# A post-norm decoder layer on one core: x1 turned by DMA, the last two feed-forwards turned by TensorE, steps ordered anew

## The reference

```
# linear attention, 16 heads of 64, 32 features
q' = exp((x Wq + bq) wq_feat);  k' = exp((x Wk + bk) wk_feat);  v = x Wv + bv
a  = q' (k'^T v) / (q' sum(k') + 1e-6);   x1 = layernorm(x + a Wproj + bproj)
# cross attention, 16 heads of 8, keys and values from the context
x2 = layernorm(x1 + softmax((x1 Wq'^T + bq')(ctx Wk'^T + bk')^T / sqrt(8)) (ctx Wv'^T + bv') Wo^T + bo)
# feed-forward 128 -> 512 -> 128 with ternary weights
h  = gelu(x2 ternary(W_fc)^T);  y = layernorm(x2 + layernorm(h; ln_w, ln_b) ternary(W_proj)^T)
```

## Time and profile before

| | us |
|---|---|
| median of 3 runs | 743.17 (742.66 to 746.18) |
| the profiled execution: its time | 746.38 |
| its span, first to last instruction | 742.9 |
| mean granted clock of TensorE | 0.972 of full speed |
| PE, DVE, ACT, POOL busy | 685.4, 527.6, 447.2, 408.5 |

### The profile page before, as it was taken

One profiled execution on the slowest core, in us unless ns is written; L12 is line 12 of the kernel. 1 busy time (PEld: TensorE's weight loads), 2 busy tenths in 40 slices (PEclk: granted clock), 3 DMA queues, 4 the chain that ended last, 5 costly groups with the idle time before them and its releaser, 6 DMA issues.

```text
span 742.9 us, 31000 instructions
## 1 busy us (share of the span) xinstructions
PE 685.4 (92%) x13506; PEld 487.3 (66%) x13506; DVE 527.6 (71%) x1476; ACT 447.2 (60%) x782; POOL 408.5 (55%) x442
## 2 busy tenths in 40 slices
...
GB/s 302 17 45 31 18 31 17 65 50 79 45 31 103 17 116 19 73 54 79 48 31 101 19 107 25 75 45 87 45 25 110 17 75 30 39 53 44 74 56 85
DMA packets 97161, 44.29 MB, mean 60 GB/s; under 512 B 87810, under 2 KB 87939, under 8 KB 96899
## 3 DMA queue, kind: packets, MB, share of 16 engines
...
...
## 4 chain that ended last, share of the span: by engine, by line
PE 72%; POOL 10%; DVE 5%; issue 5%; DMA 5%; ACT 1%; SPq 0%; POOLq 0%; DVEq 0%; ACTq 0%
PE bank L302 12%; PE bank L319 7%; PE bank L292 6%; PE bank L361 4%; DMA x2T<-x2s 4%; POOL gall L931 3%; PE bank L403 3%; PE bank L346 2%; PE bank L388 2%; POOL gs L936 2%; PE bank L315 2%; PE bank L427 2%; PE bank L434 2%; PE bank L435 2%; PE bank L339 2%
## 5 line engine op out<-in xcount | busy, mean ns | idle before, releaser
L931 POOL TENSOR_TENSOR gall<-gall,lnr 128x512 f32<-128x512 f32 x64 | 80.7, 1283 | 85.5 <-DVE st L756 85.5
L302 PE MATMUL bank<-Mh,GT 128*32 128x128 f32 x4096 | 124.4, 273 | 0.3 <-DVE GT L737 0.3
L302 PEld LDWEIGHTS bank<-Mh,GT 128*32 128x32 f32 x4096 | 110.3, 110 | 16.7 <-issue 15.3
L900 POOL TENSOR_SCALAR ve<-mv 128x4 f32<-128x4 f32 x64 | 12.4, 194 | 160.3 <-DVE mv L763 157.5
L786 DVE TENSOR_REDUCE mx<-bank 128x8 f32<-128x512 f32 x128 | 78.1, 681 | 12.6 <-PE bank L361 12.6
L737 DVE COPY GT<-bank 128x512 f32<-128x512 f32 x81 | 52.4, 682 | 36.7 <-PE bank L292 26.4
L936 POOL TENSOR_TENSOR gs<-gall,gs 128x512 f16<-128x512 f32 x64 | 73.4, 1160 | 8.4 <-ACT gs L607 8.1
L580 ACT ACTIVATE PT<-bank 128x512 f32<-128x512 f32 x128 | 64.5, 627 | 8.9 <-PE bank L388 8.9
L903 POOL TENSOR_TENSOR rstd<-ve,mhalf 128x4 f32<-128x4 f32 x64 | 66.9, 1045 | 5.3
L319 PE MATMUL bank<-Cb,qT 128*64 128x128 f32 x1024 | 66.8, 273 | 0.0
L292 PE MATMUL bank<-kp,xs 64*128 64x512 f32 x256 | 63.8, 616 | 0.0
...
## 6 DMA issues: line engine op xcount, KB each, us to landing
...
gT<-gs SPq DMA_TRANSPOSE x64, 2.8
...
```

Of the source, the lines that this page charges most:

```text
L302: m = e.matmul(bk[32 * j:32 * j + 32, tile(g_)], GT[b % 4][:, tile(hh, 32)], Mh[:, tile(hh)], start=True, stop=True)
L931: e.tensor_tensor(g[t][:, :], g[t][:, :], lnr[:, :], ALU.mult).then_inc(s_gs, 1)
```

## The change

x1 is no longer turned by PE, except for group 15. ACT casts x1 to fp16 (x1hi), POOL makes the low half (x1lo), SP turns both with one DMA transpose, and `qproj` is three fp16 matmuls with the query weights split once into halves (`xq`). For groups 14 and 15 x2 and g are turned by PE (`flip3`, and `turn` with four transposes for each of four column blocks); ACT writes the high half out of PSUM, scaled by ln_w, and DVE the low half. `gs`, `gh`, `gl` and the split in `ap2` are gone for these two. The bias that `ap2` added is a step of its own, `ab2`. The order in all three strings is new, as are some of the `+` marks. row1 now lies in a part of PT[0]; ACT's first `prob` also waits for `bias2`. The diff, cut to its core:

```diff
...
 HEAD = """
-small1 wb wk bias2 wq k0@0 k1@0 WkT zeros split@0 k2@0 mh0 g0+@0 g1@0 g2@0 g3@0 mh1 bv q0@0 nbeta q1@0 gam k3@0 small2 c0+@0 c1+@0 ks+@0 c2@0 q2@0
-kst@0 loadx@0 q3@0 WqT g4@0 g5@0 g6@0 g7@0 Wvp c3@0 Wff c4+@0 loadx@1 split@1 c5+@0 dT@0 c6+@0 xb@0 c7+@0 biasA loadc@0 bc0@0 loadx@2 bc1@0 bc2@0 bc3@0
-bias3 sbar
+wb xq wk zeros wq k0@0 small1 k1@0 bias2 q0@0 WkT k2@0 q1@0 k3@0 q2@0 split@0 nbeta gam g0+@0 WqT g1+@0 loadx@0 mh0 mh1 small2 g2+@0 bv Wvp Wff g3+@0
+g4+@0 loadx@1 g5@0 c0+@0 c1@0 ks+@0 loadx@2 c2@0 q3@0 kst@0 biasA g6+@0 g7+@0 dT@0 c3@0 c4@0 loadc@0 c5@0 c6@0 c7@0 bc0@0 split@1 bc1@0 bc2@0 bc3@0
+xb@0 sbar bias3
 PERIOD = """
-k0 k1 down0@4 k2 k3 down1@4 down2@4 score0@2 loadc score1@2 o0@1 o1@1 o2@1 o3@1 rows@2 split@-1 q0 st1@1 q1 down3@4 q2 g0+ ap2@3 g1+ xb g2+ g3 prob0@2
-gs0@3 prob1@2 ks gs1@3 ap1@1 c0+ q3 st3@4 up0@3 up1@3 kst up2@3 gl0@3 up3@3 flip@1 loadx@-2 gh0@3 gl1@3 stat@3 c1+ pv0@2 c2+ dT ap3@4 pv1@2 g4 gh1@3 g5
-g6 g7 qproj@1 kproj@1 ab1@1 gs2@3 oturn0@2 c3 c4+ c5+ c6 gh2@3 c7+ oturn1@2 gs3@3 bc0 bc1 bc2 gl2@3 gl3@3 bc3 cturn0+@2 gh3@3 cturn1+@2 vproj@1 proj0@2
-proj1@2 st2@2
+k0 k1 score0@2 score1@2 o0@1 o1@1 o2@1 o3@1 rows@2 down0@4 st1@1 down1@4 q0 ap2@3 ap1@1 k2 k3 down2@4 down3@4 split@-1 q1 g0 g1+ g2+ x1s@1 g3 st3@4
+gs0@3 prob0@2 prob1@2 gs1@3 ab2@3 ks c0 q2 up0@3 up1@3 up2@3 ap3@4 stat@3 kst up3@3 q3 gh0@3 pv0@2 c1 pv1@2 c2+ c3 dT g4+ gh1@3 g5 g6+ gl0@3 g7 gl1@3
+qproj@1 oturn0@2 gs2@3 kproj@1 oturn1@2 ab1@1 c4 gs3@3 c5 c6+ xb gh2@3 c7 bc0 bc1 bc2 gh3@3 loadx@-2 bc3 gl2@3 cturn0+@2 cturn1+@2 loadc vproj@1
+proj0@2 gl3@3 proj1@2 st2@2
 TAIL = """
...
-gl3@3 ab1@1 rows@1 ap3@4 up0@2 gs0@2 gs1@2 up1@2 up2@2 up3@2 gs2@2 down3@3 prob0@1 prob1@1 gs3@2 gh0@2 pv0+@1 gl0@2 gl1@2 stat@2 gh1@2 pv1@1 oturn0@1
-gl2@2 oturn1@1 cturn0+@1 cturn1+@1 proj0@1 proj1@1 st2@1 gl3@2 down0@2 gh2@2 ap2@1 st3@3 down1@2 gs0@1 gs1@1 gh3@2 down2@2 ap3@3 gl0@1 gl1@1 down3@2
-up0@1 gs2@1 up1@1 up2@1 gh0@1 gs3@1 up3@1 st3@2 gl2@1 gh1@1 gl3@1 stat@1 ap3@2 gh2@1 down0@1 down1@1 down2@1 down3@1 st3@1 gh3@1 ap3@1
...
+down1@3 gl2@3 vproj@1 rows@1 ab2@2 up0@2 up1@2 up2@2 down2@3 up3@2 gl3@3 prob0@1 down3@3 prob1@1 pv0+@1 st3@3 pv1+@1 stat@2 ap3@3 oturn0@1 oturn1@1
+cturn0+@1 cturn1+@1 proj0@1 proj1@1 st2@1 ab2@1 turn0@2 turn1@2 turn2@2 turn3@2 ap2@1 down0@2 down1@2 flip3@1 down2@2 down3@2 up0@1 st3@2 up1@1 up2@1
+stat@1 up3@1 turn0@1 turn1@1 turn2@1 turn3@1 ap3@2 down0@1 down1@1 down2@1 down3@1 st3@1 ap3@1
 """
...
+        flipped = {s for name, s, t, _ in PLAN if name == "flip"}
+        by_pe = sorted({s for name, s, t, _ in PLAN if name == "turn"})
...
+        x1s, x1h = sb("x1s", 1024, F16), x1T[:, :].bitcast(F16)
+        xWqh, xWql = sb("xWqh", 128, F16), sb("xWql", 128, F16)
...
+        gTc = [gTs[:, :].rearrange("p (t h c n) -> p t h c n", t=4, h=2, c=4)[:, :, :, c, :] for c in range(4)]
...
             def qproj(s):
                 bk, done = start("qproj", s)
-                w.wait_ge(*emptied("flip", s))
-                e.matmul(bk[:, :], xWq[:, :], x1T[:, :], start=True, stop=True).then_inc(done, 1)
+                if s in flipped:
+                    w.wait_ge(*emptied("flip", s))
+                    e.matmul(bk[:, :], xWq[:, :], x1T[:, :], start=True, stop=True).then_inc(done, 1)
+                else:
+                    w.wait_ge(s_xql, 1)
+                    w.wait_ge(s_x1T, 16 * (s + 1))
+                    e.matmul(bk[:, :], xWqh[:, :], x1h[:, 0:512], start=True, stop=False)
+                    e.matmul(bk[:, :], xWqh[:, :], x1h[:, 512:1024], start=False, stop=False)
+                    e.matmul(bk[:, :], xWql[:, :], x1h[:, 0:512], start=False, stop=True).then_inc(done, 1)
...
+            def flip3(s):
+                bk, done = start("flip3", s)
+                for t in range(4):
+                    w.wait_ge(s_ln["2"], 4 * s + t + 1)
+                    m = e.transpose(bk[:, tile(t)], x2[s % 2][:, tile(t)], ident[:, :])
+                m.then_inc(done, 1)
+
             def up(s, t):
                 bk, done = start("up", s, t)
                 w.wait_ge(s_prep, 6)
-                w.wait_ge(s_x2T, 16 * (s + 1))
+                if s in by_pe:
+                    w.wait_ge(*emptied("flip3", s))
+                else:
+                    w.wait_ge(s_x2T, 16 * (s + 1))
                 e.matmul(bk[:, :], x2T[:, tile(t)], tfc[:, :], start=True, stop=False)
                 e.matmul(bk[:, :], x2T[:, tile(4 + t)], tfc[:, :], start=False, stop=True).then_inc(done, 1)
 
+            def turn(s, c):
+                bk, done = start("turn", s, c)
+                for t in range(4):
+                    w.wait_ge(*emptied("up", s, t))
+                    m = e.transpose(bk[:, tile(t)], g[t][:, tile(c)], ident[:, :])
+                m.then_inc(done, 1)
+
             def down(s, t):
                 bk, done = start("down", s, t)
-                w.wait_ge(s_gT[t], 16 * (s + 1))
+                if s in by_pe:
+                    for c in range(4):
+                        w.wait_ge(*emptied("turn", s, c))
+                else:
+                    w.wait_ge(s_gT[t], 16 * (s + 1))
...
+            def xq():
+                w.wait_ge(s_small2, 16)
+                e.activation(xWqh[:, :], xWq[:, :], ACT.Copy).then_inc(s_xqh, 1)
+
+            def x1hi(s):
+                w.wait_ge(s_ln["1"], 4 * s + 4)
+                if s > 0:
+                    w.wait_ge(s_x1T, 16 * s)
+                e.activation(x1s[:, 0:512], x1[s % 2][:, :], ACT.Copy).then_inc(s_x1h, 1)
...
+            def flip3(s):
+                if s > 0:
+                    w.wait_ge(*filled("up", s - 1, 3))
+                w.wait_ge(*filled("flip3", s))
+                e.activation(x2T[:, 0:512], bank[uses["flip3", s, 0][0]][:, :], ACT.Copy).then_inc(s_x2hp, 1)
...
+            def turn(s, c):
+                if s > 0:
+                    w.wait_ge(*filled("down", s - 1, 3))
+                w.wait_ge(*filled("turn", s, c))
+                b3 = bank[uses["turn", s, c][0]][:, :].rearrange("p (t n) -> p t n", t=4)
+                e.activation(gTc[c][:, :, 0, :], b3, ACT.Copy, scale=lnw[:, c:c + 1]).then_inc(s_ghp, 1)
...
+                w.wait_ge(s_x2hp, by_pe.index(s) + 1)
+                e.tensor_tensor(x2T[:, 512:1024], bank[uses["flip3", s, 0][0]][:, :], x2T[:, 0:512], ALU.subtract).then_inc(emptied("flip3", s)[0], 1)
...
+            def turn(s, c):
+                w.wait_ge(s_ghp, 4 * by_pe.index(s) + c + 1)
+                b3 = bank[uses["turn", s, c][0]][:, :].rearrange("p (t n) -> p t n", t=4)
+                e.scalar_tensor_tensor(gTc[c][:, :, 1, :], b3, lnw[:, c:c + 1], gTc[c][:, :, 0, :], ALU.mult, ALU.subtract).then_inc(emptied("turn", s, c)[0], 1)
...
+            def x1lo(s):
+                w.wait_ge(s_ln["1"], 4 * s + 4)
+                w.wait_ge(s_x1h, s + 1)
+                e.tensor_tensor(x1s[:, 512:1024], x1[s % 2][:, :], x1s[:, 0:512], ALU.subtract).then_inc(s_x1l, 1)
...
+
+            def ab2(s):
+                if s in by_pe:
+                    w.wait_ge(*filled("flip3", s))
+                    w.wait_ge(s_ln["2"], 4 * s + 4)
+                else:
+                    w.wait_ge(s_x2l, s + 1)
                 w.wait_ge(*emptied("bias3", 0))
-                addbias(x, x, bias3).then_inc(s_x2b, 1)
+                addbias(x2[s % 2], x2[s % 2], bias3).then_inc(s_x2b, 1)
...
+            def x1turn(s):
+                w.wait_ge(s_x1l, s + 1)
+                if s > 0:
+                    w.wait_ge(*filled("qproj", s - 1))
+                e.dma_start(x1h[:, :].rearrange("p (n c) -> p n c", n=8), x1s[:, :], transpose=True).then_inc(s_x1T, 16)
```

More of the change, by code:

```diff
@@ L28 @@
 WIDE = {"score": 4, "prob": 4, "mh": 2}
-BANKED = "k q ks kst dT bc g c o flip kproj vproj qproj score rows prob pv oturn cturn proj up down wq wk wb mh biasA bias2 nbeta gam bias3 sbar".split()
-WHOLE = "small1 small2 ab1 st1 st2 st3 ap1 ap2 ap3 bias2 bias3".split()
+BANKED = "k q ks kst dT bc g c o flip kproj vproj qproj score rows prob pv oturn cturn proj flip3 up turn down wq wk wb mh biasA bias2 nbeta gam bias3 sbar".split()
+WHOLE = "small1 small2 x1s flip3 ab1 ab2 st1 st2 st3 ap1 ap2 ap3 bias2 bias3".split()
@@ L47 @@
[L47 to L50, removed]
@@ L51 @@
-gl3@3 ab1@1 rows@1 ap3@4 up0@2 gs0@2 gs1@2 up1@2 up2@2 up3@2 gs2@2 down3@3 prob0@1 prob1@1 gs3@2 gh0@2 pv0+@1 gl0@2 gl1@2 stat@2 gh1@2 pv1@1 oturn0@1
-gl2@2 oturn1@1 cturn0+@1 cturn1+@1 proj0@1 proj1@1 st2@1 gl3@2 down0@2 gh2@2 ap2@1 st3@3 down1@2 gs0@1 gs1@1 gh3@2 down2@2 ap3@3 gl0@1 gl1@1 down3@2
-up0@1 gs2@1 up1@1 up2@1 gh0@1 gs3@1 up3@1 st3@2 gl2@1 gh1@1 gl3@1 stat@1 ap3@2 gh2@1 down0@1 down1@1 down2@1 down3@1 st3@1 gh3@1 ap3@1
+k0@1 score0@3 ap2@4 score1@3 k1@1 q0@1 o0@2 o1@2 o2@2 o3@2 st1@2 rows@3 gs0@4 q1@1 k2@1 ap1@2 k3@1 up0@4 down0@5 down1@5 x1s@2 up1@4 down2@5 gs1@4
@@ new lines @@
+up2@4 up3@4 g0@1 g1@1 g2+@1 g3@1 down3@5 prob0@3 prob1@3 ab2@4 gl0@4 stat@4 gh0@4 gh1@4 c0+@1 c1@1 st3@5 pv0@3 ks+@1 pv1@3 gs2@4 qproj@2 oturn0@3 q2@1
```

(13 more changed lines are left out.)

58 lines of the change are left out of this document (41 added, 17 removed).

## The result

The changed kernel took 747.49 us (median of 19 runs, 741.68 to 750.76), the kernel before 743.06 (19 runs, 741.54 to 747.19): ratio 1.0051, 95% interval 1.0032 to 1.0070. The forecast of 718.2 us, with a range of 708 to 731, was wrong: the kernel is half a per cent slower and not 3.4% faster.

A forecast was written before the change was run, and what follows sets the result against it. PE's queue was taken to bound the periods, latency the tail; 11.2 + 1.8 - 2.0 + 1.0 + 0.8 + 2.4 + 9.8 = 25.0 us off the profiled 746.38, from the median 718.2 us, range 708 to 731.

The forecast's parts named there:

- x1 by DMA, PE slots: Per group on PE: `flip` and fp32 `qproj` (1.49 us) give way to three fp16 matmuls (0.69); 14 x 0.80 = 11.2 us gained.
- x1's chain costs nothing: Period: x1's halves and DMA transpose land near 18.5 us, `qproj` comes near 28.9; ten microseconds of slack, cost 0.
- x2T waits: Period, PE at `up`: waits for x2T of 3.6 us over five; half taken as gain, 1.8 us, bounds 0 to 3.6.
- (c) of the order: Period: DVE must finish bc products, x2 sums and statistics before the eight maxima; charged 0.15 us a period, +2.0 us, bounds 0 to 14.
- No engine overtakes PE: Period: new loads per group of DVE 34.1, ACT 26.3, POOL 26.5 us stay below a period of 40.9.
- What PE idle costs: Steady periods: time is the sum of PE's slots; DVE lateness was charged in us per period, 0.15, bounds 0 to 1.
- Head: Start of kernel: WqT loaded third, so PE's 0.99 us wait for it goes; gain about 1.0 us, bounds -2 to 3.
- Tail: End of kernel: group 14's `qproj` 0.8, stretch to the last `proj` 2.4, stretch after it 9.8 us gained.
- Up to the last `proj`: Tail's first part: group 14's `qproj` gains 0.80 us; o3 of group 15 to its `proj` gains 2.4, bounds -3 to 6.
- behind it: After the last `proj`: PE turns replace POOL work and DMA; 38.3 us become 28.5, gain 9.8, alternatives 5 to 14.
- B: Rival: new waits eat the period's gain, `cturn` and `proj` having little slack; period stays near 41.75, 729.4 us; chance 0.20.
- C: Rival, slower: ACT's gh3, ahead of both cturn copies, makes PE late at proj0; decides from 1.8 us a period; 760; chance 0.08.

## Why the prediction was wrong

The sum was head 1.0, period 11.2 + 1.8 - 2.0, tail 0.8 + 2.4 + 9.8. Measured at the `bc` cuts: head 2.2, periods -17.8, tail 13.2. By its steps:

- *x1 by DMA, PE slots*: right. `qproj` is 0.65 us as forecast, and PE busy in a period at full clock is 40.0 to 40.2.
- *x1's chain costs nothing*: right in the new order (the transpose is issued at 425.42 and `qproj` comes at 441.82); wrong in the old one as soon as POOL's queue holds x1's low half behind a wait, which two experiments showed.
- *x2T waits*: all gone, within the bounds of 0 to 3.6.
- **The failed step is (c) of the order, DVE's charge of 0.15 us a period**: "My walk has it there within a few tenths". It measured 1.79 us of PE idle, and on average some 1.1 us more of PE time at the lower clock, 13.9 us in all. The upper bound I gave for it (14 us, 1 us a period) was too low by half: against the kernel whose split is late, the two together are 29.9 us. In the walk, which the prediction doesn't print, I gave each scaling its price alone, some 0.28 us, so eight were 2.3. They took 4.89, because `ap1` now stands right behind `ap2`, and its four run beside POOL's two splits (3.71 us). The row that should have set the price was in my own list: 3.35 us for four beside POOL work, which I used for the tail and not here. "No engine overtakes PE" added up loads (34.1 of 40.9, measured 34.5) and was true; the load said nothing of the moment at which one bank came free.
- *What PE idle costs*: the prediction priced a wait at its own length. Here 1.79 us of it cost 3.5 where the clock fell behind it (1.79 + 1.7), and 1.8 where it did not.
- *Head*: 2.2 for 1.0, inside its bounds. The new head was not run alone.
- *Tail*: 13.2 for 13.0, by errors that cancel. Up to the last `proj` it gained 1.1 and not 3.2 (97.17 from 98.31 us), behind it 12.06 and not 9.8: the clock was granted 0.77 over the stretch, for 0.58 before, and 1.00 from 731.50 to 735.66, where nearly all turns of the last group's g run, so `down` began at 16.6 and not 18.3. Sixteen turns took 1.91 us (L467), 0.12 each. The 390 ns of the Trainium skill (VectorE: DVE Perf Modes, The three transpose paths) do not appear here either; the measurement decides.
- *Rivals*: B (new waits eat the gain) had the right kind, but priced it at 11.2 us where it measured 29.9, and looked for it at `cturn` and `proj`. C (slower) was the right sign at the wrong place: no wait at `proj`, no lateness of gh3. Its turning point holds: it decides from 1.8 us a period, and 29.9 over 13 is 2.3.

With that wait mended the number comes out: 718.81 and 717.88 us against a forecast of 718.2. In part that is luck. By the cuts, the kernel with the late split gains 4.1 us in the head (forecast 1.0), 10.3 in the 13 periods (11.0 for 14), 13.1 in the tail (13.0) over the trace of the kernel before. The 10.3 is made up otherwise than I had it. PE's busy time fell by 8.8 (0.80 a period would be 10.4). The wait at L397 still costs 6.1, where I had 2.0. And 7.6 us of other PE idle time went, where I had 1.8: the x2T waits (3.6) and nearly all of the gap in `pv` (5.4 before, 0.2 now), which I had taken as given, because its releaser is "issue" and no other engine is waited for. How much of this a second trace of the kernel before would show is open: the run with the old period and the new tail had 7.6 us of idle in its periods and not 12.5.

So the place of `split@-1` decided whether the gain arrived, but the parts are not worth the terms of the sum each: x1 by DMA in the old order brought next to nothing.

One more thing stays open: why the clock held behind four of the twelve waits, which were as long as the others. It is not the length alone: with x1 by DMA in the old order the clock fell behind two of the twelve waits for x1T of more than 1 us (2.16 and 2.50 us, granted 0.66 over the next 5 us) and held behind the others, of 1.22 to 1.94 us.
